# A two-layer kernel on one core: scan tables as outer products of short ones, and another order of the first steps

## What is computed

```
r = abs(phazor_c)
p = tanh(r) * exp(1j * angle(phazor_c))
prog = p[None, :] ** arange(L)[:, None]            # L = 256
conv = causal convolution of x with prog, plus last_conv_c * prog * p
return conv.real
```

## Time and profile before

| | us |
|---|---|
| median of three runs | 327.61 |
| lowest and highest of them | 326.7, 327.82 |
| the profiled execution, its own time | 326.35 |
| its span | 324.5 |
| PE busy | 290.7 (90%) |
| DVE busy | 219.3 (68%) |
| GpSimd (POOL) busy | 151.6 (47%) |
| ScalarE (ACT) busy | 121.5 (37%) |

### The profile page before, as it was taken

How to read it: one execution, slowest core, us unless ns; L and a number is a source line. 1 busy time by engine, 2 the same in 40 slices (tenths; PEclk the granted TensorE clock), 3 DMA queues, 4 the chain that set the end, 5 groups by cost and what they waited for, 6 DMA issues and landing times.

```text
span 324.5 us, 4438 instructions
## 1 busy us (share of the span) xinstructions
PE 290.7 (90%) x1514; PEld 188.9 (58%) x1514; DVE 219.3 (68%) x454; ACT 121.5 (37%) x195; POOL 151.6 (47%) x161
## 2 busy tenths in 40 slices
PE   0886597979899999999899798997899999999995
PEld 0654254736446564656456464554558888888784
DVE  4687899898867779666866766678977851234313
ACT  1672172354563303153452536203104662036510
POOL 3578143759625220225534454426055795019920
PEclk9999697999999999999999999999999999999999
DMA  6964343445530001301000111110002000110003
GB/s 204 362 207 167 97 120 124 146 131 163 165 128 34 12 20 35 97 2 44 8 26 25 32 32 34 32 32 0 3 0 68 1 0 2 65 65 2 1 0 129
DMA packets 12262, 22.85 MB, mean 70 GB/s; under 512 B 1360, under 2 KB 1872, under 8 KB 12240
## 3 DMA queue, kind: packets, MB, share of 16 engines
q1 hardware_dynamic: 12240, 22.57, 22.1%
HBM read 20.46 MB, written 2.10 MB: 70 GB/s over the span
## 4 chain that ended last, share of the span: by engine, by line
PE 69%; DVE 15%; POOL 7%; issue 5%; ACT 2%; DMA 1%; SPq 0%; DVEq 0%; ACTq 0%; POOLq 0%
PE bank L719 10%; PE bank L625 10%; PE bank L626 10%; PE bank L595 8%; PE bank L593 8%; PE bank L594 8%; PE bank L679 4%; PE bank L658 2%; PE bank L652 2%; PE bank L587 2%; DVE lno L958 2%; DVE uscan L976 2%; POOL root L1081 2%; PE bank L670 1%; POOL hidl L1139 1%
## 5 line engine op out<-in xcount | busy, mean ns | idle before, releaser
L1139 POOL TENSOR_TENSOR hidl<-hid,hidh 128x512 f16<-128x512 f32 x28 | 34.5, 1233 | 65.1 <-ACT hidh L785 65.1
L625 PE MATMUL bank<-xh,gatew 128*128 128x512 f16 (+1 forms) x124 | 45.0, 373 | 1.6 <-DVE xl L914 1.1
L626 PE MATMUL bank<-xl,gatew 128*128 128x512 f16 (+1 forms) x124 | 45.0, 373 | 0.0
L625 PE MATMUL bank<-xh,upw 128*128 128x512 f16 (+1 forms) x124 | 44.6, 369 | 0.4 <-ACT upw L811 0.4
L626 PE MATMUL bank<-xl,upw 128*128 128x512 f16 (+1 forms) x124 | 44.2, 366 | 0.0
L719 PE MATMUL bank<-downw,hidh 128*128 128x512 f16 x112 | 42.5, 379 | 0.0
L719 PE MATMUL bank<-downw,hidl 128*128 128x512 f16 x112 | 42.4, 379 | 0.0
L1081 POOL TENSOR_TENSOR root<-var,powers 128x4 f32<-128x4 f32 (+1 forms) x25 | 24.6, 983 | 38.2 <-DVE var L947 29.5
L847 ACT ACTIVATE silu<-bank,early 128x512 f32<-128x512 f32 x28 | 19.3, 688 | 56.5 <-PE bank L626 56.5
L1145 POOL TENSOR_TENSOR actl<-hid,acth 128x512 fp32r<-128x512 f32 (+1 forms) x22 | 28.4, 1297 | 22.5 <-ACT acth L792 22.4
L1049 DVE SCALAR_TENSOR_TENSOR hid<-bank,early,silu 128x512 f32<-128x512 f32 (+1 forms) x22 | 16.5, 751 | 17.4 <-ACT silu L862 15.8
(11 more groups left out here) (142 smaller groups left out, 643.1 us busy)
## 6 DMA issues: line engine op xcount, KB each, us to landing
stage<-in_gate SPq DMA_DIRECT2D x14, 256.0 KB, 3.5
stage<-in_up SPq DMA_DIRECT2D x14, 256.0 KB, 2.8
stage<-in_down SPq DMA_DIRECT2D x14, 256.0 KB, 2.9
X<-in_x SPq DMA_DIRECT2D x8, 256.0 KB, 6.5
out_x<-X SPq DMA_DIRECT2D x8, 256.0 KB, 2.0
stage<-in_v SPq DMA_DIRECT2D x6, 256.0 KB, 2.6
stage<-in_mask SPq DMA_DIRECT2D x4, 256.0 KB, 3.0
stage<-in_weight SPq DMA_DIRECT2D x4, 256.0 KB, 2.6
```

The costliest lines, as they stand in the source:

```text
L625: pe.matmul(bank_of(key)[:, c], w, xh[b][:, k, c], start=(k == 0), stop=False)
L626: mm = pe.matmul(bank_of(key)[:, c], w, xl[b][:, k, c], start=False, stop=(k == KT - 1))
L1139: pool.tensor_tensor(hidl[:, n % FT, :], hid[:, n % UNITS, :], hidh[:, n % FT, :], ALU.subtract).then_inc(hid_lo, 1)
```

## The change

**Tables.** Two short tables, `fine` (powers 0 to 16 of the phasor) and `coarse` (powers of its 16th power), are grown by GpSimd alone, in four doublings each of three steps: one product of all four pairs (`prod`), a difference and a sum. `turned` lays out the coarse one with signs for the lower and upper 64 partitions. The table of a depth is then an outer product: two products of 16x16 and their sum (`outer`). DVE does it for depth 0 behind `tables_ready`, GpSimd for depths 1 to 3 behind slots 4, 6 and 8. `rot` holds one part per partition, so `lower` is gone. ScalarE's step with tanh comes behind the last `first`.

**Seed.** GpSimd's seed is cut into four pieces, each behind the root of one token tile.

**Low part from PSUM.** `xl` is PSUM minus xh. The float32 copy is a step of its own, `xcopy`, which waits for xl; bank and projection wait for it (`xt_copied`). Block 1's tiles move one slot ahead, and LN_AT up to two.

**Loads.** `early` and the first four weight tiles are issued by ScalarE's queue, the four token tiles stand first on SP's. A one-element SiLU (`warm`) loads ScalarE's function table at the start.

```
-    for i in range(GROWTHS):
-        for part in range(4):
-            after[GROW_AT[i] + (part if i == GROWTHS - 1 else 0)].append(("grow", i, part))
-    after[GROW_AT[-1] + 3].append(("lower",))
+    for l in range(DEPTH):
+        after[TABLE_AT[l]].append(("table", l))
     for t in range(TPB):
         after[XT_AT + XT_STEP * t].append(("xt", 1, t))
+        after[XT_AT + XT_STEP * t + 1].append(("xcopy", 1, t))
...
-            order += [("stats", 0, 0, t), ("root", 0, 0, t, 1)]
+            order += [("stats", 0, 0, t), ("root", 0, 0, t, 1), ("seed", t)]
...
+        if 3 <= t:
+            order.append(("xcopy", 0, t - 3))
...
+    order += [("decay",)] + [("grow", i) for i in range(GROWTHS)] + [("turn",)]
...
-LN_AT = (1, 2, 3, 3, 3, 5, 5, 6, 8)
-XT_AT, XT_STEP = 5, 2
+LN_AT = (1, 1, 2, 2, 2, 4, 4, 5, 6)
+XT_AT, XT_STEP = 4, 2
+ROOTN = 16
-POOL_GROWTHS = 6
-GROW_AT = (0, 0, 0, 0, 0, 0, 3, 4)
+TABLE_AT = (3, 4, 6, 8)
...
+        def outer(eng, l, part, work):
+            n = [P, ROOTN, ROOTN]
+            dst = rot[:, l, :].rearrange("p (a c) -> p a c", a=ROOTN)
+            tmp_ = rot_t[:, work, :].rearrange("p (a c) -> p a c", a=ROOTN)
+            if part == 2:
+                return eng.tensor_tensor(dst, dst, tmp_, ALU.add)
+            return eng.tensor_tensor(tmp_ if part else dst, turned[:, part, l, :].unsqueeze(2).to_broadcast(n),
+                                     fine[:, l, 0:ROOTN, part].unsqueeze(1).to_broadcast(n), ALU.mult)
...
-            for t in range(1, TPB):
+            for t in range(TPB):
                 sp.dma_start(X[:, t, :], x[t]).then_inc(x_in[t], 16)
-            for n in range(4):
-                load(n)
...
+            act.dma_start(early[:], params).then_inc(prm_in, 16)
+            for n in range(FIRST_LOADS):
+                kind, i = casts[n]
+                act.dma_start(stage[:, n, :], source[kind][i]).then_inc(stage_in[n], 16)
+            act.wait_ge(pool_chain, 1)
+            act.activation(warm[:], powers[:, 0, 0:1], ACT.Silu)
...
-                    act.activation(xh[b][:, :, c], src, ACT.Copy)
-                    act.activation(XT[:, :, c], src, ACT.Copy).then_inc(xt_hi, 1)
+                    act.activation(xh[b][:, :, c], src, ACT.Copy).then_inc(xt_hi, 1)
+                elif kind == "xcopy":
...
+                    act.wait_ge(xt_lo, b * TPB + t + 1)
+                    src = bank_of(("xt", b, t))[:].rearrange("p (k n) -> p k n", k=KT)
+                    act.activation(XT[:, :, t * P:(t + 1) * P], src, ACT.Copy).then_inc(xt_copied, 1)
...
-                    emit(dve.tensor_tensor(xl[b][:, :, c], XT[:, :, c], xh[b][:, :, c], ALU.subtract), xt_lo)
+                    src = bank_of(step)[:].rearrange("p (k n) -> p k n", k=KT)
+                    emit(dve.tensor_tensor(xl[b][:, :, c], src, xh[b][:, :, c], ALU.subtract), xt_lo)
...
+                    half, i = divmod(step[1], GROWTHS // 2)
+                    table, n = (fine, coarse)[half], 1 << i
+                    if half == 1 and i == 0:
+                        link(pool.tensor_copy(coarse[:, :, 1, :], fine[:, :, ROOTN, :]))
+                    link(pool.tensor_tensor(prod[:, :, :, 0:n, :].rearrange("p l a t c -> p l a (t c)"),
+                                            known, nth, ALU.mult))
...
+                elif kind == "table" and step[1] > 0:
+                    for part in range(2):
+                        link(outer(pool, step[1], part, 1))
+                    outer(pool, step[1], 2, 1).then_inc(table_ready, 1)
```

More of the change, by code:

```diff
@@ L53 @@
 EPS = 1e-5
+FIRST_LOADS = 4
 NSTAGE = 6
@@ L170, in build_order @@
     placed = [step for slot in after for step in slot]
-    assert placed.index(("lower",)) < placed.index(("scan", 0, 0))
-    order = [("seed",)]
+    assert all(placed.index(("table", l)) < placed.index(("scan", 0, l)) for l in range(DEPTH))
+    order = []
     for t in range(TPB + 3):
         if t < TPB:
-            order += [("stats", 0, 0, t), ("root", 0, 0, t, 1)]
+            order += [("stats", 0, 0, t), ("root", 0, 0, t, 1), ("seed", t)]
         if 1 <= t <= TPB:
@@ L181, in build_order @@
             order.append(("xt", 0, t - 2))
-        if 2 <= t <= 3:
-            order.append(("cast", ("gate", "up")[t - 2], 0))
+        if 3 <= t:
+            order.append(("xcopy", 0, t - 3))
+        if t == 2:
+            order += [("cast", kind, 0) for kind in ("gate", "up")]
         if 3 <= t:
             order.append(("first", t - 3))
+    order += [("decay",)] + [("grow", i) for i in range(GROWTHS)] + [("turn",)]
     order += [("cast", k, 1) for k in ("gate", "up")] + [("rows",)]
@@ L567, in _ @@
                 sp.dma_start(X[:, t, :], x[t]).then_inc(x_in[t], 16)
-            for n in range(4, 12):
+            for n in range(FIRST_LOADS, 12):
                 load(n)
@@ L812, in _ @@
                                    ACT.Copy).then_inc(codes_ready["act"], 1)
-                elif kind == "seed":
+                elif kind == "decay":
                     act.wait_ge(size_ready, 1)
@@ L921, in _ @@
                                            ALU.subtract), yt_lo)
-                elif kind == "grow" and step[1] >= POOL_GROWTHS:
-                    if step[1:] == (POOL_GROWTHS, 0):
-                        dve.wait_ge(tables_ready, 1)
-                    emit(growth(dve, *step[1:]), hold=step[2] % 2 == 1)
+                elif kind == "table" and step[1] == 0:
+                    dve.wait_ge(tables_ready, 1)
+                    for part in range(3):
+                        emit(outer(dve, 0, part, 0), hold=part > 0)
                 elif kind == "rows":
@@ L933, in _ @@
                     emit(dve.memset(onesr[:].bitcast(F32), 1.0 / DIM), row_ready)
-                elif kind == "lower":
-                    dve.wait_ge(tables_ready, 1)
-                    emit(dve.tensor_copy(rot[DIM:P, :, 0, :], rot[DIM:P, :, 1, :]))
                 elif kind == "ln":
@@ L1085, in _ @@
                 kind = step[0]
-                if kind == "seed":
+                if kind == "seed" and step[1] == 0:
                     re, im = col("re", 0, DEPTH), col("im", 0, DEPTH)
@@ L1093, in _ @@
                     link(pool.tensor_tensor(s2, s2, c0, ALU.add))
-                    pool.tensor_tensor(size, s2, powers[:, 1, :], ALU.pow).then_inc(size_ready, 1)
-                elif kind == "grow" and step[1:] == (0, 0):
-                    pool.wait_ge(size_ready, 1)
                     link(pool.tensor_scalar(zero, s2, 0.0, None, ALU.is_equal))
+                elif kind == "seed" and step[1] == 1:
                     link(pool.tensor_tensor(re1, re, zero, ALU.add))
@@ L1100, in _ @@
                     link(pool.tensor_tensor(inv, zero, powers[:, 0, :], ALU.pow))
+                elif kind == "seed" and step[1] == 2:
+                    pool.tensor_tensor(size, s2, powers[:, 1, :], ALU.pow).then_inc(size_ready, 1)
                     link(pool.tensor_scalar(im1, im, -1.0, None, ALU.mult))
[L1103 to L1105 removed]
@@ L1106, in _ @@
-                    link(pool.memset(rot[:, :, 1, 0:1], 0.0))
-                    link(pool.tensor_tensor(c0, rot[:, :, 0, 1], col("lc_p", 0, DEPTH), ALU.mult))
+                    link(pool.tensor_tensor(fine[:, :, 1, 0], re1, inv, ALU.mult))
+                    link(pool.tensor_tensor(fine[:, :, 1, 1], im1, inv, ALU.mult))
+                elif kind == "seed":
+                    for start in (fine, coarse):
+                        link(pool.memset(start[:, :, 0, 0:1], 1.0))
+                        link(pool.memset(start[:, :, 0, 1:2], 0.0))
+                    link(pool.tensor_tensor(c0, fine[:, :, 1, 0], col("lc_p", 0, DEPTH), ALU.mult))
```

65 lines of the change are left out of this document (35 added, 30 removed).

## The result

| | before | with the change |
|---|---|---|
| median of four runs each, us | 327.37 | 321.63 |
| lowest and highest | 326.7, 327.82 | 320.05, 322.12 |
| profiled execution, its own time | 326.35 | 321.57 |
| its span | 324.5 | 319.7 |

The ratio is 0.9833, with a 95% interval of 0.9807 to 0.9859: the kernel is faster, by 5.5 us at this ratio where 7.8 were forecast. The two medians by themselves lie 5.7 us apart; the ratios in this document are the ones on record, and not quotients of the medians beside them. The predicted 319.8 lies 1.8 us under the median. Further down, the ratios leave out slow executions (one of k_slots, three of t_late), while the medians hold all.

What follows compares the result with a forecast made beforehand. PE, busy 90% of the span, was taken as the bound through its idle time and low clock. Terms 0.4 + 2.9 + 2.9 + 1.6 = 7.8 us off the median 327.61 gave 319.8, range 317.0 to 324.0.

Steps and rivals of the forecast that it cites:

- Start: PE's first stretch: 1.1 us won by xl from PSUM, 0.7 lost by token tile 1 landing later; net +0.4.
- Hidden, 0: ScalarE's start: one table load instead of two; the second was over before PE's first unit was ready, so worth 0.
- Short tables on POOL: POOL's seed done at 16.1, then 24 growth steps of 4 to 128 elements; `tables_ready` at 26.7 against 27.9.
- DVE's table: DVE behind `tables_ready`: three steps of 256 elements instead of four larger ones, 2.0 us (1.4 to 2.6), done at 28.8.
- First gap: PE's idle time before block 1's first transpose: 3.4 us instead of 6.3, gain 2.9.
- Clock: PE's low clock behind its gaps: 1.7 us lost instead of 4.6, gain 2.9 (1.2 to 4.6).
- Second gap: PE's wait before the first scan's result: 0.8 us instead of 2.4, gain 1.6.
- The rest of the kernel: Behind block 1's input projection (L643): time won for PE up to its end is won for the kernel.
- My signs: Right: `tables_ready` 26 to 28, longest gap 3 to 4, L643 near 54.6; wrong: POOL steps above 0.5, later gap above 1.8.
- given back later: Rival: DVE sets the pace from 60 to 90, PE waits elsewhere; 1 us or less left, 326.9; chance 0.05.
- The clock stays: Rival: PE's clock stays at 2.4 GHz through the 3.4 us gap; gain 10.0, 317.6; chance 0.17.
- Slower: Rival: POOL pays for the interleaved layout; gain gone at 0.58 a step, 332.9 at the dearest row; chance 0.04.

Runs made afterwards that it cites:

- k_slots: The changed kernel with block 1's norms and transposes in their old slots, the transpose behind unit 2's `up`: 321.79 us, ratio 0.9833.
- t_late: The changed kernel with POOL's tables of depths 1 to 3 behind slots 11, 18 and 22 instead of 4, 6 and 8: 328.29 us, ratio 1.0023.
- t_none: The changed kernel with the tables of depths 1 to 3 left out and filled with ones: 321.89 us, ratio 0.9854.
- fill14: The changed kernel with 14 matmuls of 512 columns ahead of block 1's first transpose, which overwrites their result: 320.21 us, ratio 0.9809.
- k_oneq: The changed kernel with all first loads on SP's queue again, in the order of before: 320.75 us, ratio 0.9806.
- x_only: The kernel before with only xl read from PSUM and XT's copy as its own step behind it: 327.09 us, ratio 1.001.
- t_only: The changed kernel with loads, seed, xl and block 1's slots as before, so only the tables and `warm` are new: 326.97 us, ratio 0.9997.
- oq_fill: k_oneq with 12 matmuls of 512 columns ahead of block 1's first transpose, which overwrites their result: 319.59 us, ratio 0.9781.
- no_tab: The kernel before with everything of the change but the tables; the cast of `up` also stays in its old place: 325.53 us, ratio 0.9968.
- oq_fill_early: oq_fill with POOL's tables of depths 1 to 3 behind slots 3, 4 and 6 instead of 4, 6 and 8: 320.3 us, ratio 0.9802.

## Why the prediction was right, and where it was not

The direction and the range (317.0 to 324.0) held. The likeliest case, a gain of 6 to 9 us, was just missed with 5.5 (5.7 by the medians), and the sum was 7.8 for a span that shrank by 4.8. Term by term:

- **Start: +0.4 forecast, 1.85 measured in this trace, 1.1 to 1.9 in five.** k_slots, t_late, t_none and fill14 have the same first steps as the change and reach unit 1 at 17.07, 17.83, 17.89 and 17.62 (18.99 before). Part of the 1.85 is therefore chance: PE's matmuls became faster at 12.75 here and at 14.6 before. Where that moment lies at 14.57 to 14.84, as in t_late, t_none and fill14, the gain is 1.1 to 1.4. The token tiles: X1's statistics start at 5.07 instead of 5.58 (5.15 to 5.51 in those four), so the 0.7 that I took off was wrong in sign. Tile 2 came later in this execution (its statistics at 7.80, after a wait of 1.06), but in none of those four (6.88 to 7.22, no wait). The Trainium skill ("DMA: Bandwidth & Descriptors", Issuing engines are not separate DMA queues) says that a second issuing engine saves only issue time; by this rule I had put the loss at 1.7. The rule agrees with k_oneq, but my 1.7 from it does not: X1 gained 0.1 to 0.5, at most about the earlier issue. The waits of xl: 0.41 and 0.64 instead of 1.52 and 1.15 here, 1.6 together where I took 1.1, but a part of this is the clock again, since xl also waits for PE's transpose. The cast of `up`: PE's wait of 0.37 for it is gone, because the change moved it, which I had not priced. And the table load, "Hidden, 0": it was hidden behind a delay that the change itself removes (x_only).
- **Short tables on POOL: 26.7 forecast, 24.43 measured.** The seed was done at 14.26 instead of 16.1, since nine of its small steps take 0.20 or 0.21; the growth took 10.2, as forecast (10.55). That this is no less than the long steps needed was in my numbers too, and I did not draw the conclusion: the tables alone do nothing for `tables_ready` (t_only).
- **DVE's table: 2.0 forecast, 1.84 measured. First gap: +2.9 forecast, +2.6 measured.** XN began at 29.44, 1.1 us earlier than forecast, and PE's `gate` ended 1.35 earlier. Both ends moved nearly alike.
- **Clock: +2.9 forecast, +2.73 measured.** The first low stretch took 3.46 us of PE, the second did not come. This is right by luck: I left the second out because its gap was to be under 1 us. The gap was 2.46, as long as the 2.39 that was followed by 0.52 before, and in this execution no low stretch followed. Another of the four has a mean clock of 0.982, another 1.00.
- **Second gap: +1.6 forecast, -0.1 measured, with two new waits of 0.65 and 0.67.** This is the step that failed. I let DVE run from the end of the table to the first scan in 17.5 us; it took 20.7 (26.74 to 47.48). I had about 2 us in this for waits on PE and for two hits by POOL's tables, "at most 1 us each". The waits alone were 2.75 (1.39 for xh, 1.36 for PE's bank). The tables come on top: t_none puts 2.0 us on them, directly and by what they delay, and in t_late the same stretch is 3.2 us shorter (30.71 to 44.81); t_only, where they stand beside the same scan, shows the same 2.62. That the tables made the gap is thus shown. What it costs in time is not: t_none has hardly a gap and no better median.
- **The rest of the kernel: 0 forecast, -0.88 measured.** I argued that time won up to the end of L643 is time won for the kernel. 85% of it was. Of DVE's steps between the projection's end and 64.61 one differs from before: `var`, 1.16 instead of 0.65, which is the 0.5 us of that gap; the other 0.4 I did not find in one place.
- **My signs.** Of those for being right, PE's longest gap (3.69) held; `tables_ready` came at 24.4 instead of 26 to 28, the gap before the first scan was not under 1, and L643's second run ended at 56.68, not near 54.6. Of those for being wrong, two came: a gap between 60 and 100 over 1.8 (2.32), and POOL steps above 0.5, though not in the growth but in the tables of depths 1 to 3 (0.62 to 1.05).

Of the rivals, *given back later* is the one that took a part. *The clock stays* was also real: one of the four runs of the change has a mean clock of 1.00, and it is the fastest, 320.05. *Slower* had the right engine and the wrong price: POOL's interleaved growth steps cost 0.20 to 0.46 each.

Right as a sum is not right as a reason. The errors had both signs: +1.45 at the start, a good part of it chance, against -0.3, -0.2, -1.7, -1.3 for the two new waits and -0.9 in the rest. And my ledger added the parts. The runs show that they are worth 5.5 us together and 1.1 when each half is measured on its own, the cast of `up` aside.

## What to carry to other kernels

When two engines feed one wait, price the edits together: draw for each edit which of the two comes last with and without the other edit. A step that costs nothing because something covers it must be priced again if another part of the same change removes the cover. Work moved to an idle engine is not free where it runs beside the busy one (the first scan took 2.62 us, and 2.26 with POOL's tables left out; the multiply before it 1.65, and 0.69), nor when it stands in that engine's order ahead of a step on the path (t_late).

## What was not expected of the hardware

The length of an idle piece does not tell whether PE's clock falls behind it. In oq_fill PE waits 2.45 us and then runs at 0.57 over four us; in fill14 it waits 2.45 us at the same place and the clock stays at 1.00. oq_fill, then fill14:

```profile
46.50:50.50 4.00, 4.00 (x15) 1.77 (x15) 3.22 (x7) 2.71 (x6) 1.15 (x1) 0.57 0.45 104
```

```profile
46.00:50.00 4.00, 4.00 (x23) 2.28 (x24) 3.25 (x6) 2.56 (x5) 1.12 (x2) 1.00 0.32 83
```

In x_only a gap of 1.84 before 59.32 was followed by 1.7 us at 1.00 and then, from 61, by 7.5 us at 0.54; in k_slots one of 1.84 before 54.59 by none. And equal executions of the change had mean clocks from 0.982 to 1.00. A low stretch of one profile is a price with a chance, not a fixed cost.

At the start the granted clock reads 1.00 while PE's matmuls of 128 columns still take 0.31 us, and 0.22 later. The switch came at 14.6 before, at 12.75 with the change and at 17.05 in no_tab, whose PE began at 7.09. What sets it was not tested. With the first steps of the change it lay between 12.75 and 14.84, and unit 1 began between 17.07 and 17.89. k_oneq, oq_fill and oq_fill_early, alike among themselves, switched at 14.75, 12.53 and 15.66 and began unit 1 at 17.80, 16.90 and 18.71. So the start of a single trace can be off by a microsecond or more, as much as the parts that are weighed here.
